# A fused cross-attention and feed-forward kernel: the keys' matmuls taken chunk by chunk of W_k's rows, and the vector engine's work around the first pair of tiles written in another order

## The reference, cut to what matters

```python
# 8 heads of 128; J = 2 * 77 = 154 keys
q, k, v = layernorm(x) @ Wq, ctx @ Wk, ctx @ Wv        # Wq 512x1024, Wk and Wv 384x1024
sim = (q @ k.T) * 128 ** -0.5                          # per head
sim = (sim - mean(sim)) * 1.5 + mean(sim)
x = x + softmax(sim) @ v @ Wout + bout                 # Wout 1024x512
y = layernorm(x)
y_prev = y shifted down by one row in each batch       # first row: zeros
r = sigmoid((mu_r * y + (1 - mu_r) * y_prev) @ W_r.T)
k = (mu_k * y + (1 - mu_k) * y_prev) @ W_k.T
out = x + r * (square(relu(k)) @ W_v.T)                # W_r, W_k, W_v 512x512
```

## Time and profile before

| | |
|---|---|
| median of 3 runs | 752.24 us (752.21 to 752.44) |
| the profiled execution, its own time | 752.19 us |
| its span, first to last instruction | 750.4 us |
| PE busy | 741.4 us, 99% of the span |
| DVE, ACT, POOL busy | 511.0, 425.3, 121.3 us (68%, 57%, 16%) |
| share of the chain that ended last | PE 84%, DVE 5%, ACT 4%, DMA 3% |
| TensorE's granted clock | full in every slice |

### The profile page before, as it was taken

The page is one execution under the profiler, slowest core; times in us unless marked ns, Lnnn a source line. Parts: engine busy times, 40 slices in busy tenths (PEclk is TensorE's granted clock), DMA queues, the critical chain, the costliest instruction groups (busy, mean ns, idle before and its releaser), DMA issues.

```text
span 750.4 us, 13618 instructions
## 1 busy us (share of the span) xinstructions
PE 741.4 (99%) x3996; PEld 647.1 (86%) x3996; DVE 511.0 (68%) x1073; ACT 425.3 (57%) x1204; POOL 121.3 (16%) x279
## 2 busy tenths in 40 slices
PE   8999999989999999999999999999999999999998
PEld 7976888888888889898988989898888988888887
DVE  2667777677776766667767666777766677776662
ACT  3677557464655657464664755466475646555432
POOL 1110001212112121212102121210202121020211
PEclk9999999999999999999999999999999999999999
DMA  9933534544445444543444454444435444343301
GB/s 301 370 115 113 173 95 148 168 142 128 146 139 167 122 134 147 161 146 108 152 129 140 129 170 137 130 138 134 152 103 175 133 149 140 117 147 103 109 30 43
DMA packets 85017, 106.54 MB, mean 142 GB/s; under 512 B 9824, under 2 KB 61818, under 8 KB 84988
## 3 DMA queue, kind: packets, MB, share of 16 engines
q1 hardware_dynamic: 84148, 105.36, 44.8%
q10 hardware_dynamic: 839, 0.83, 0.4%
HBM read 58.70 MB, written 47.45 MB: 141 GB/s over the span
## 4 chain that ended last, share of the span: by engine, by line
PE 84%; DVE 5%; ACT 4%; DMA 3%; issue 2%; SPq 1%; POOL 1%; ACTq 0%; POOLq 0%; DVEq 0%
PE ffn L485 11%; PE ffn L487 11%; PE ffn L486 11%; PE scores L486 8%; PE scores L487 8%; PE scores L485 8%; PE attended L487 7%; PE attended L486 7%; PE attended L485 7%; ACT probs L772 1%; DMA wk<-in_L_xattn_Wk 1%; ACT probs L781 1%; DMA handed<-x_rows 1%; DMA x_rows<-normed 1%; PE attended L523 1%
## 5 line engine op out<-in xcount | busy, mean ns | idle before, releaser
L486 PE MATMUL scores<-A_lo,xT_hi 128*128 128x462 f32 (+1 forms) x384 | 134.6, 350 | 0.0
L485 PE MATMUL scores<-A_hi,xT_hi 128*128 128x462 f32 (+1 forms) x384 | 134.2, 349 | 0.0
L487 PE MATMUL scores<-A_hi,xT_lo 128*128 128x462 f32 (+1 forms) x384 | 134.1, 349 | 0.0
L772 ACT ACTIVATE probs<-scores,neg_max 128x154 f32<-128x154 f32 x256 | 96.4, 389 | 38.3 <-DVE neg_max L1044 37.9
L487 PE MATMUL attended<-B_hi,pT_lo 128*128 128x512 f32 x288 | 112.4, 390 | 0.0
L486 PE MATMUL attended<-B_lo,pT_hi 128*128 128x512 f32 x288 | 112.3, 390 | 0.0
L485 PE MATMUL attended<-B_hi,pT_hi 128*128 128x512 f32 x288 | 112.0, 389 | 0.0
L1044 DVE TENSOR_REDUCE neg_max<-scores 128x3 f32<-128x462 f32 (+1 forms) x96 | 54.9, 583 | 74.6 <-PE scores L487 74.5
L1316 POOL TENSOR_SCALAR var<-stats 128x1 f32<-128x1 f32 x64 | 12.2, 191 | 470.0 <-DVE stats L991 468.9
L485 PEld LDWEIGHTS scores<-A_hi,xT_hi 128*128 128x128 f32 x384 | 72.4, 189 | 7.3 <-issue 0.8
L486 PEld LDWEIGHTS scores<-A_lo,xT_hi 128*128 128x128 f32 x384 | 72.3, 188 | 5.8
(11 more groups left out here) (177 smaller groups left out, 1528.3 us busy)
## 6 DMA issues: line engine op xcount, KB each, us to landing
prob_rows<-probs SPq DMA_DIRECT2D x32, 704.0 KB, 3.4
probs_handed<-prob_rows SPq DMA_DIRECT2D x128, 176.0 KB, 3.3
x_rows<-normed SPq DMA_DIRECT2D x61, 256.0 KB, 2.1
handed<-x_rows SPq DMA_DIRECT2D x244, 64.0 KB, 1.9
x_in<-in_x SPq DMA_DIRECT2D x32, 256.0 KB, 3.5
out<-x SPq DMA_DIRECT2D x31, 256.0 KB, 2.5
wq<-in_L_xattn_Wq SPq DMA_DIRECT2D x4, 512.0 KB, 9.9
wout<-in_L_xattn_Wout SPq DMA_DIRECT2D x1, 2048.0 KB, 14.7
```

The source lines that it names most:

```text
L485: te.matmul(psum, left[0], right[0], start=first, stop=False)
L486: te.matmul(psum, left[0], right[1], start=False, stop=False)
L487: return te.matmul(psum, left[1], right[0], start=False, stop=last)
L772: last = nc.scalar.activation(probs[:, q, cols], S[b][:, (h - h0) * J:(h - h0 + 1) * J], ACT.Exp, bias=neg_max[:, h:h + 1], accum_out=row_ ...
```

## The change

Three things are changed. W_k is loaded in three chunks of 128 whole rows (4096 bytes each), all by SP, and PE runs over the chunk outermost: each chunk's products for all eight heads are added up in the three banks, which are all complete only with the third chunk. W_q comes in two loads of four heads (pieces of 2048 bytes). DVE takes the even heads of `wqT` and ACT the odd ones. For the first pair, `mix` is divided into `mix_change` (the difference) and `mix` (one of `xk`, `xr`), and the order written out by hand is changed on DVE, ACT and SP. The repeated `step` issues the same instructions as before, but for `hand_x2(2)`, which now waits for `x_turn(5)` where it waited for `x2_turn(1)`.

```diff
-        wk_loaded = [sem(f"wk_loaded{i}") for i in range(5)]
-        wq_loaded = [sem(f"wq_loaded{i}") for i in range(4)]
+        wk_loaded = [sem(f"wk_loaded{i}") for i in range(CC)]
+        wq_loaded = [sem(f"wq_loaded{i}") for i in range(2)]
...
@@ -314,9 +314,6 @@
...
-        wk_rows = Wk.rearrange("(c p) n -> p c n", p=P)
-        KEY_LOADS = [(0, 1), (1, 2), (2, 3), HEAD_BANKS[1], HEAD_BANKS[2]]
...
-            for i in (0, 2, 4):
-                load_keys(i)
-            for i in range(4):
-                cols = slice(2 * i * P, 2 * (i + 1) * P)
+            for c in range(CC):
+                sp.dma_start(wk[:, c, :], Wk[c * P:(c + 1) * P, :]).then_inc(wk_loaded[c], 16)
+            for i in range(2):
+                cols = slice(4 * i * P, 4 * (i + 1) * P)
                 sp.dma_start(wq[:, :, cols], wq_rows[:, :, cols]).then_inc(wq_loaded[i], 16)
...
-                    sp.wait_ge(xn2T_ready, 1 if isinstance(t, int) and t == 5 else t - 3)
+                    sp.wait_ge(xn2T_ready, 2 if isinstance(t, int) and t == 5 else t - 3)
...
-                    sp.wait_ge(x_turned, t + 5)
-                elif is_tile(t + 3) and not (isinstance(t, int) and t == 2):
+                    sp.wait_ge(x_turned, 5)
+                    if begun(t - 1):
+                        sp.wait_ge(xn2T_ready, t)
+                elif is_tile(t + 3):
...
             hand_x2(0)
             store_probs(3)
             load_x(5, 1)
-            hand_x(5)
             store_x2(1)
             hand_x2(1)
             hand_probs(3)
+            hand_x(5)
             turns(sp, step)
...
-            for b, (h0, h1) in enumerate(HEAD_BANKS):
-                for h in range(h0, h1):
-                    te.wait_ge(wk_loaded[min(h, 3) if h < EARLY else 4], 16)
-                    for c in range(CC):
+            for c in range(CC):
+                te.wait_ge(wk_loaded[c], 16)
+                for b, (h0, h1) in enumerate(HEAD_BANKS):
+                    for h in range(h0, h1):
                         last = te.matmul(S[b][:, (h - h0) * J:(h - h0 + 1) * J], wk[:, c, h * P:(h + 1) * P],
-                                         ctxT[:, c, :], start=(c == 0), stop=(c == CC - 1))
-                last.then_inc(keys_done, 1)
+                                         ctxT[:, c, :], start=(c == 0 and h == h0), stop=(c == CC - 1 and h == h1 - 1))
+                    if c == CC - 1:
+                        last.then_inc(keys_done, 1)
...
             for h in range(HEADS):
-                te.wait_ge(wq_loaded[h // 2], 16)
+                te.wait_ge(wq_loaded[h // 4], 16)
...
-            load_keys(1)
-            load_keys(3)
...
-            for h in range(0, HEADS, 2):
+            for h in range(1, HEADS, 2):
                 act_e.wait_ge(wq_turned, h + 1)
-                copy(wqT[:, h, :], WQ_BANKS[h % len(WQ_BANKS)][:]).then_inc(wqT_even_ready, 1)
+                copy(wqT[:, h, :], WQ_BANKS[h % len(WQ_BANKS)][:]).then_inc(wqT_odd_ready, 1)
...
             x2_norm(1, 1)
             for i in range(3):
                 probs_hi(2, i)
+            for w in "kr":
+                mixed_high(w, 0, 0)
+            for b in range(3):
+                exponentials(4, b)
+            mixed_high("k", 1, 1)
+            normalise_early(4)
             x_hi(5)
-            mixed_high("k", 0, 0)
-            mixed_high("r", 0, 0)
-            mixed_high("k", 1, 1)
-            exponentials(4, 0)
             mixed_high("r", 1, 1)
-            exponentials(4, 1)
-            exponentials(4, 2)
-            normalise_early(4)
+            open_gate(0, 0, 2)
             pack_hi(4)
-            open_gate(0, 0, 2)
             x2_norm(2, 2)
             for i in range(3):
                 probs_hi(3, i)
...
+            def mix(w, t, half, pair):
+                before = slice(half * P, (half + 1) * P)
+                change = mixed_change(t, half)
                 dve.wait_ge(delta_ready, t + 1)
...
-                    mix(t - 1, 1 - half, pair)
+                    mix_change(t - 1, 1 - half, pair)
+                    for w in "kr":
+                        mix(w, t - 1, 1 - half, pair)
...
-            for h in range(1, HEADS, 2):
+            for h in range(0, HEADS, 2):
                 dve.wait_ge(wq_turned, h + 1)
-                v.tensor_copy(wqT[:, h, :], WQ_BANKS[h % len(WQ_BANKS)][:]).then_inc(wqT_odd_ready, 1)
+                v.tensor_copy(wqT[:, h, :], WQ_BANKS[h % len(WQ_BANKS)][:]).then_inc(wqT_even_ready, 1)
...
             add_x(1, 0, 1)
             x2_turn(0, 0, 0)
             probs_turn(2)
+            mix_change(0, 0, 0)
             for i in range(3):
                 probs_lo(2, i)
-            x_turn(5)
             dve.wait_ge(mu_loaded, 32)
-            mix(0, 0, 0)
-            mixed_low("k", 0, 0)
-            mixed_low("r", 0, 0)
-            x2_turn(1, 1, 0)
-            mix(1, 1, 0)
-            mixed_low("k", 1, 1)
+            for w in "kr":
+                mix(w, 0, 0, 0)
             for b in range(3):
                 maxima(4, b)
+            for w in "kr":
+                mixed_low(w, 0, 0)
+            x2_turn(1, 1, 0)
+            mix_change(1, 1, 0)
+            mix("k", 1, 1, 0)
+            inverse_early(4)
+            mixed_low("k", 1, 1)
+            add_x(2, 0, 2)
+            normalise_late(4)
+            x_turn(5)
+            mix("r", 1, 1, 0)
             x_lo(5)
             mixed_low("r", 1, 1)
-            inverse_early(4)
-            normalise_late(4)
             pack_lo(4)
-            add_x(2, 0, 2)
             probs_turn(3)
             for i in range(3):
                 probs_lo(3, i)
```

More of the change, by code:

```diff
@@ L328, in load_rows @@
                 sp.dma_start(dst[:], src.rearrange("(c p) n -> p c n", p=P)).then_inc(loaded, 16)
-            def load_keys(i):
-                cols = slice(KEY_LOADS[i][0] * P, KEY_LOADS[i][1] * P)
-                sp.dma_start(wk[:, :, cols], wk_rows[:, :, cols]).then_inc(wk_loaded[i], 16)
             def load_x_in(i):
@@ L1074, in add_x, with mixed_change, mix_change @@
                 statistics(x2[slot], raw2, stats2, raw2_ready, stats2_ready, t)
-            def mix(t, half, pair):
-                into = 1 - half
+            def mixed_change(t, half):
+                return x_view(normed) if is_last(t) else delta[1 - half][:]
+            def mix_change(t, half, pair):
                 cols, before = slice(1 + half * P, 1 + (half + 1) * P), slice(half * P, (half + 1) * P)
@@ L1084, in mix @@
                     dve.wait_ge(halo_zeroed, 1)
-                change = delta[into][:]
                 if is_last(t):
                     dve.wait_ge(xn_stored, 16 * (TILES - 2))
-                    change = x_view(normed)
                 elif begun(t - 3):
                     dve.wait_ge(out_ready, t - 2)
-                v.tensor_tensor(change, xn2T[:, :, cols], xn2T[:, :, before], ALU.subtract).then_inc(delta_ready, 1)
-                dve.wait_ge(delta_ready, t + 1)
-                for w in "kr":
-                    if begun(pair - 1):
-                        if w == "r":
-                            dve.wait_ge(r_done, t - 1)
-                        else:
-                            dve.wait_ge(k_done, 2 * pair)
-                    for c in range(DC):
-                        last = v.scalar_tensor_tensor(out=mixed[w][:, c, before], in0=change[:, c, :],
-                                                      scalar=mu[w][:, c:c + 1], in1=xn2T[:, c, before],
-                                                      op0=ALU.mult, op1=ALU.add)
-                    last.then_inc(mixed_ready[w], 1)
+                v.tensor_tensor(mixed_change(t, half), xn2T[:, :, cols], xn2T[:, :, before], ALU.subtract
+                                ).then_inc(delta_ready, 1)
+            def mix(w, t, half, pair):
+                before = slice(half * P, (half + 1) * P)
+                change = mixed_change(t, half)
+                dve.wait_ge(delta_ready, t + 1)
+                if begun(pair - 1):
+                    if w == "r":
+                        dve.wait_ge(r_done, t - 1)
+                    else:
+                        dve.wait_ge(k_done, 2 * pair)
+                for c in range(DC):
+                    last = v.scalar_tensor_tensor(out=mixed[w][:, c, before], in0=change[:, c, :],
+                                                  scalar=mu[w][:, c:c + 1], in1=xn2T[:, c, before],
+                                                  op0=ALU.mult, op1=ALU.add)
+                last.then_inc(mixed_ready[w], 1)
             def mixed_low(w, t, half):
```

3 lines of the change are left out of this document (removed).

## The result

| | before | changed |
|---|---|---|
| median, same job | 753.72 us (752.21 to 753.9, 7 runs) | 750.35 us (748.79 to 751.0, 7 runs) |
| the profiled execution | 752.19 us, span 750.4 | 749.69 us, span 747.9 |

The ratio of the changed kernel's time to that of before is 0.9957, 95% interval 0.9947 to 0.9968: 3.2 us faster. The forecast was 4.3 us faster, at 747.9. The kernel before measured 1.5 us higher in this job than in the three runs shown ahead; why it has two groups of times is one of the things that the experiments settle.

The account below looks back on a forecast made before the run. PE bounds the kernel, fully busy from 153 to 700 us, so only set-up and PE's waits can give: 752.19 - 1.4 (set-up) - 0.36 - 2.57 (two `xk_lo` waits) = 747.9 us, range 747.1 to 750.3.

Parts of the forecast that it names:

- The loads come sooner: Set-up: W_k as whole rows moves at 398 GB/s from 4 us on, so A starts 1.4 us sooner.
- the dip: Set-up, 4 to 6 us: transfers at only 153 GB/s, laid to W_k's short column pieces.
- The rival that held the dip to belong to any program's start: Set-up: the pieces do not cause the slow transfers, part one gains nothing, 749.3 us; chance 0.16.
- the keys end at 5.75 + 6.46 = 12.2: Set-up: 48 key records on PE at 0.135 us each, ending at 12.2 instead of 13.51.
- The forecast of 16.1: End of the set-up: A starts at 16.1 instead of 17.49, a gain of 1.4 us.
- The first wait, 0.36 us: First pair: PE's wait for `xk_lo` at 106.48 goes, worth 0.36 us.
- The 2.57 us go too, with 0.8 to spare: Pair 1: PE's wait for `xk_lo` at 152.44 goes; it ends at 148.7, PE asks at 149.5.
- `handed` for tile 5: First pair: lands at 106.3, DVE asks at 107.9; landing at 108.7 or later would keep the second stall.
- The shift of 3.6 us: DVE reaches `pT` of tile 3 3.6 us earlier, handed down a chain to `x_norm(7)` and the second `xk_lo`.
- the landing of tile 2's `x2`: SP's queue: `hand_x2(2)` waits for `x_turn(5)` at 108.5, long before its store at 112, costing nothing.
- The rival of a stall that stays: Pair 1: the stall at 152 stays wholly or in part, around 750.0 us (full loss 750.4); chance 0.12.

Follow-up runs that it names:

- `columns_one_queue`: The kernel before with all five column loads of W_k issued by SP, none by ACT; 751.77 us, one run.
- `peeled`: The kernel before with PE's first loop round (tiles 4 to 7) written out ahead of the loop, a control; 753.78 us, ratio 1.0006.
- `keys_only`: The kernel before with only the new loads, loop order and copies of the set-up; 753.13 us, ratio 0.9992.
- `filled`: `peeled` with nine idle identity products on PE ahead of the wait for `xk_lo` of pair 1; 752.15 us, ratio 0.9991.
- `pair_only`: The kernel before with only the new order around the first pair; 750.92 us, ratio 0.9968.
- `rows_two_queues`: The changed kernel with the second of W_k's three whole-row chunks issued by ACT in its own queue; 749.95 us, one run.
- `load_first`: The changed kernel with tile 6's x load issued right ahead of the store of tile 4's probabilities, not 5 us earlier; 750.89 us, ratio 0.9966.
- `early_load`: The changed kernel with tile 6's x load moved 5 us ahead, before the store of tile 4's probabilities; 748.87 us, ratio 0.9942.
- `wq_three`: `early_load` with W_q in three loads of four, two and two heads, for two loads; 749.52 us, ratio 0.9952.
- `changed_look`: A later execution of the changed kernel, unchanged, run once more for its trace; 748.92 us, one run.

## Why the prediction was right or wrong

It had the direction and the place of the gain, and the time came out 0.05 us above its range. The time measured behind A's start separates the two parts. Each line is the profiled execution's time less the start of A in it, so that the set-up drops out:

| kernel | time - A | A's start |
|---|---|---|
| before | 752.19 - 17.49 = 734.70 | 17.49 |
| `columns_one_queue` (order of before) | 734.29 | 17.48 |
| `peeled`, `keys_only` (order of before, clock fell) | 735.72, 735.89 | 18.05, 18.14 |
| `filled` (order of before, PE kept busy) | 733.87 | 18.63 |
| `pair_only` | 732.95 | 17.96 |
| the changed kernel, three profiles | 732.92, 733.08, 732.97 | 16.77, 16.43, 15.95 |
| `rows_two_queues` | 733.10 | 16.85 |
| `load_first` | 732.68 | 18.21 |
| `early_load`, `wq_three` | 731.67, 731.79 | 16.48, 18.14 |

**The loads come sooner: right.** Whole rows filled the dip for the greater part (313 to 332 GB/s over 2 to 6 us in the changed kernel's three profiles for 223; 402 over 9 to 14 for 349). The rival that held the dip to belong to any program's start is out; its argument that the length of the pieces does not make the engines idle did not decide, for with columns they were idler, whatever the reason. The Trainium skill's rule that spoke against this part (*DMA: Bandwidth & Descriptors*, Specifications: line rate from 512 bytes on) isn't borne out here: W_q moved at 349 GB/s with pieces of 1024 bytes against 402 with 2048, at a share of 1.10 and 1.06, and the median packet of 512 bytes took 27 ns where one of 4096, eight times as long, took 159.

**"the keys end at 5.75 + 6.46 = 12.2", and A at 16.1: a term that was mis-sized.** 0.135 us a record was taken from the last 30 records in before's profile and laid on all 48. That is PE's full pace, which it has only from some moment on, and ahead of it the key records are 0.257 us apart. In before's profile the moment was 4.5 us, ahead of the keys, so the rows could not show it. In the changed kernel's three profiles it was 4.9, 4.9 and 7.0, in `rows_two_queues` and `early_load` 4.4 and 4.1, and in the other seven, of both set-ups, 8.5 to 9.9. Where it came early the new set-up has A at 15.95 to 16.85, up to 1.5 us sooner than before's 17.49. Where it came late the new set-up has A at 18.14 to 18.21 and the old one at 17.48 to 18.63: nothing gained, since PE's slow records take the time in which the old kernel would have waited for W_k (from the first key to W_q's transposes 8.3 us with the new loads, 7.6 to 8.5 with the old). The forecast of 16.1 was met in one profile of the changed kernel.

`keys_only` measured -0.6 +/- 0.8 us where 1.4 was forecast, but it met the fall of the clock in 11 of its 12 runs, before in 13 of 22. Among the runs with the fall alone its mean is 752.96 us and that of before 753.95, so the set-up is worth some 1.0 us on average: about 2 us in 4 of the 11 (751.58 to 751.93), little in the other 7 (753.01 to 754.11). Why the fall came more often there was not found.

**The first wait, 0.36 us: right**, in all profiles of the new order.

**"The 2.57 us go too, with 0.8 to spare": this step failed.** `handed` for tile 5, the link that the rival had named, was there in time. The shift of 3.6 us was there at `pT` of tile 3, where the working had put it. It was then handed down a list in which ACT, DVE, POOL and SP's `hand_x(6)` stood, but not tile 6's own load, nor the landing of tile 2's `x2`, which the prediction had set at "nothing". Both wait in SP's queue for their turn, and there the change did not move everything by the same amount. Before, the three issues stood at 113.29, 113.90 and 117.20, the load landed after 4.4 us and the store of `x2` after 2.0, and DVE never waited for the load. The change brought `x2_norm(2)` forward so far that all three are issued within 0.9 us, and the landings grew to 5.7 and 5.9. Of the 3.6 us, `x_norm(7)` got 1.82 (141.45 for 143.99, less 0.72), and 1.23 us of the stall stayed. The rival of a stall that stays in part came true, by SP's queue. This is shown by `early_load`: with the load out of that heap the time behind A is 731.67, which is 3.03 below before and 2.62 below `columns_one_queue`; the forecast for this part was 0.36 + 2.57 = 2.93. The Trainium skill has a completion land only after every earlier write of the same DMA engine (*DMA: Bandwidth & Descriptors*, Queues, rings and completion order); the trace agrees in that the landing goes with the bytes ahead, 2.6 us alone and 5.7 behind 704 KB, though it doesn't show the order of single writes.

**What the forecast lacked.** A stall was costed at its idle time. In 29 of 56 executions of before it costs 1.5 us more, through the clock. Removing half of it took away the whole of that: in all five profiles with 1.07 to 1.26 us idle the granted clock stayed at 1.00, and none of the 33 runs of the changed kernel, `pair_only`, `load_first` and `rows_two_queues` has a mean clock below 1.0. That the shorter length is what spares the clock is argued from these counts; no run varied the length alone. This made up for what the heap in the queue and the set-up did not give: the sum by the traces is -2.5, the medians differ by 3.4, with before's median an execution that has the fall.

So the time, 750.35, lies 2.45 us above the forecast for two reasons. Behind A it is 733.0 in all its profiles where the forecast comes to 734.70 - 2.93 = 731.8: 1.2 us, the stall that the heap in the queue kept. And 750.35 - 733.0 puts A's start in the median run at 17.4 instead of 16.1: 1.3 us, most of it PE's slow first records by the traces above, worked out and not seen, since no trace of that run was taken. That the gain over before in the same job, 3.2 us, comes nearer to the forecast 4.3 than 752.24 - 750.35 = 1.9 does is luck: it holds the fall of the clock, which the forecast did not have.

## What to carry to other kernels

When a chain is moved forward, go through the issuing queue as through an engine: list which transfers will now stand in it at one time, and give each the landing time of all the bytes ahead, not its own. A load whose buffer is long free belongs ahead of that heap; here a change of four lines bought another 1.3 us behind A (2.0 us between the medians). And a stall of PE of about two microseconds can cost more than its length, so halving one can pay more than the time that it takes off; where a kernel's times come in two groups, look at the granted clock behind its stalls first. A pace read late in a set-up need not hold at its start, and one profile of a start is one draw of several.

## What the runs showed of the hardware

- **The clock after a short stall.** With 1.8 and 2.05 us idle the granted clock fell from 2.4 to 1.2 GHz for some 3.4 us in two profiles; with 1.9 and 2.42 it did not in two others; with 1.07 to 1.26 it did in none of five, and not with 0.89 in one. The fall began after PE had resumed: the first three matmuls behind the stall were still at full pace. Sixteen matmuls at 0.213 us for 0.12 cost 1.5 us. The Trainium skill (*TensorE: Matmul & The Clock Gate*, Part 1, HAM oscillation) warns of idle gaps longer than these; here shorter ones were enough in about half of the runs.
- **PE's first records.** Until 4.1 to 9.9 us, by the execution, PE runs at half its pace: 9 records of the keys take 2.52 us in `keys_only` where 18 take 2.52 in `changed_look`. The column of the granted clock shows 1.00 for both, but the trace's first entry of the clock stands at 9.87 us in the one, the moment at which its records turn from 0.257 to 0.13 us apart, and at 4.91 in the other, ahead of all its key records. Before the first entry the column is 1.00 for want of one. The same page of the Trainium skill has the engine begin slow and be released by activity, and the number of slow matmuls at a kernel's start vary from run to run; both fit. What sets the length was not found.
- **Landings add up in one queue.** 256 KB land after 2.6 us alone, 3.0 right ahead of 704 KB, 4.0 behind it, and 5.7 and 5.9 as the two behind it. Whether the queue or the DMA engines behind it set this was not tested.
